# A new prologue for a two-layer attention and expert kernel: loads, splits, masks, sines and the first rotation in another order and place, and later x splits moved within their steps

## The chip, the cores and the metric

The kernel runs on one NeuronCore of a Trainium2 chip. Five engines run their own instruction streams and meet at semaphores: TensorE (PE), VectorE (DVE), ScalarE (ACT), GpSimd (POOL) and SyncE (SP), which here only issues DMAs. The metric is the device time of one execution in microseconds (us). Weights, activations and caches lie in HBM in float32.

## The reference, cut to what matters

For 8 batches of 128 tokens with 512 features, the first layer is attention over 512 cached and 128 new keys, with 32 query heads that share 8 key/value heads, and the second a linear layer with two gated low-rank experts per token.

```
q, k, v = x @ Wq.T, x @ Wk.T, x @ Wv.T            # 32 query heads, 8 key/value heads, D = 128
q, k = rmsnorm(q, q_norm_w), rmsnorm(k, k_norm_w)
pos = cache_seqlens[:, None] + arange(128)
q, k = rope(q, pos), rope(k, pos)                  # sines and cosines of pos * inv_freq
k_all = concat(k_cache[block_table], k); v_all = concat(v_cache[block_table], v)
scores = einsum(q, k_all) / sqrt(D); cached keys from cache_seqlens on are masked
x = x + softmax(scores) @ v_all @ Wo.T
x = x + x @ W.T + 2 * sum over the top 2 of 8 experts: gate * (x @ A_e.T) @ B_e.T
```

## The kernel before, in words

**Precision.** Every float32 matmul operand is split into a high part (a copy by ACT into the type float32r) and a low part (full minus high, by DVE, line 664). A product is three passes: high by high, low by high, high by low (lines 280 to 282). So all weights, x, queries, keys, probabilities and values go through ACT once and DVE once. The tiles have `_hi` and `_lo` in their names.

**Steps.** The work is numbered by g = 8 h + b, for key/value head h and batch b: 64 of them, one step each. It is software-pipelined by hand: step s computes the scores, softmax and transposed probabilities of g = s; the rotated queries and keys of g = s + 1; the projections Q and KV of g = s + 2; and the output of g = s - 1 (`O`, then `Y`, which DVE adds to the tile y, line 807). The loop runs from s = -2, so steps -2 and -1 are the prologue, and the text calls "step s" the stretch from the first scores matmul of step s (line 1011) to that of step s + 1. The order on every engine is the order of the code. Twelve outputs of PE a step (the list UNITS: `O`, `T0`, `Q` and so on) share the 4 PSUM banks of `ps_w` in turn.

**A step's loop over engines.** PE makes scores for 4 query heads; DVE takes each head's row maximum with the mask added (L727); ACT the exponential (L527); DVE the reciprocal of the sum (L734); ACT scales (L533); PE transposes (L1034); ACT and DVE split the transposed result (L538, L664). Beside it POOL takes the inverse norms for the next g (meansq L415, rstd L417, wr = norm weight times rstd L420), DVE scales by wr (u, L783), POOL multiplies by the cosine (L427), DVE by the sine (m2, L790), POOL adds the two halves (L434), and PE transposes the rotated queries (QT, L1102), the cached keys (KTC, L1019) and the new keys (KTN, L1113). Then the scores of the next step can start. POOL also issues four indirect DMAs per g that gather cached keys and values (L406).

**Weights of the next head.** W_AT and WO_AT say in which step a piece of the next head's weights is split: ACT at the end of step s (L478, L486), just ahead of the copy of KTN, DVE in step s + 1 after the second reciprocal; SP loads the piece a step before, as soon as DVE has freed the ring slot.

**x.** The transposed x of batch g is split once in head 0, kept in HBM (`keep_x`) and fetched again for later heads. The x of 4 batches is staged in half of y; when its splits are done, the natural x of those 4 batches is loaded over it (`natural_x`, L340), since Y is added to it.

**The prologue before.** Steps -2 and -1 hold all else that is done once: position angles and their reduction modulo 2 pi (L855 to L873), sines (L508, L509), masks of all 8 batches (L691), language biases (L697, 8 small ones), the splits of head 0's weights, which are loaded into tiles of later use, and the split of the first output weights wo (L493). ACT's order is: copy Q(0), two splits of wo, copy KV(0), squares. The gathers of g = 0 and 1 are issued by POOL ahead of all its arithmetic. ACT's copy of Q(1) (L589) waits for all 8 masks, because the key numbers from which they are made lie in the tile `raw`.

## Time and profile before

| | |
|---|---|
| median of 3 runs | 1195.59 us (1194.82 to 1195.92) |
| the profiled execution | 1195.48 us |
| its span (first to last instruction) | 1193.7 us |
| PE busy / DVE / ACT / POOL | 1155.7 / 928.4 / 938.9 / 768.2 us |
| first scores matmul | 34.66 us into the span |

The profile is of one execution. "Busy" for PE is modelled from pipelined matmuls. "Idle before, releaser" names the instruction whose semaphore ended a wait. A row of the timeline gives the start from the span's beginning, the duration, the engine, the line of the kernel and the operation. DVE and POOL instructions have their own records, so a duration that is much above that of its kind is read as a wait inside the instruction.

### The profile page before, as it was taken

How to read it: one execution, taken by the hardware profiler on the slowest of the kernel's cores; microseconds unless marked ns; L12 is line 12 of the kernel's file. 1: busy time of each engine (PE TensorE's matmuls, PEld its weight loads, DVE VectorE, ACT ScalarE, POOL GpSimd, SP SyncE). 2: the span in 40 equal slices, each digit the busy share in tenths (PEclk: the TensorE clock that was granted, in tenths of full speed). 3: DMA queues.
4: the chain of work that ended last, by engine and by line, in shares of the span. 5: the costliest groups of instructions: out<-in, count | busy, mean ns of one | idle time of the engine just before them, and what ended most of it. 6: DMA issues, size and time to landing. Idle time of an engine off the chain costs nothing.

```text
span 1193.7 us, 20774 instructions
## 1 busy us (share of the span) xinstructions
PE 1155.7 (97%) x6912; PEld 1025.5 (86%) x6912; DVE 928.4 (78%) x1880; ACT 938.9 (79%) x1830; POOL 768.2 (64%) x838
## 2 busy tenths in 40 slices
PE   3799999999999999999999999999999999999998
PEld 2688888888888888888888888888888888888787
DVE  6788887787878777887877787778878777877746
ACT  3787888888888888888888888888888888888741
POOL 5566666667677667676776766667667667666500
PEclk9899999999999999999999999999999999999999
DMA  6322412221222122122213222231222122121001
GB/s 237 119 85 96 146 61 80 94 93 48 93 94 76 64 93 94 53 88 93 90 51 94 93 67 74 93 94 49 92 93 81 58 92 91 55 69 54 18 1 71
DMA packets 53626, 98.11 MB, mean 82 GB/s; under 512 B 8592, under 2 KB 25872, under 8 KB 53264
## 3 DMA queue, kind: packets, MB, share of 16 engines
q1 hardware_dynamic: 41232, 63.21, 15.1%
q0 software_dynamic: 12288, 33.57, 9.5%
q8 instruction: 57, 0.93, 0.3%
q14 instruction: 49, 0.40, 0.1%
HBM read 90.45 MB, written 6.29 MB: 81 GB/s over the span
## 4 chain that ended last, share of the span: by engine, by line
PE 85%; DVE 5%; ACT 5%; issue 3%; DMA 1%; SPq 1%; POOL 0%; DVEq 0%; POOLq 0%; ACTq 0%
PE ps_s L1011 18%; PE ps_w L282 16%; PE ps_w L281 16%; PE ps_w L280 16%; PE ps_w L1034 8%; PE ps_w L1119 2%; PE ps_w L1102 2%; PE ps_s L993 2%; PE ps_w L1019 2%; ACT ps L527 2%; DVE pt_lo L664 2%; ACT ps L533 1%; DVE ps L727 1%; DMA y<-wo 1%; ACT pt_hi L538 1%
## 5 line engine op out<-in xcount | busy, mean ns | idle before, releaser
L406 POOL DMA_INDIRECT kv_raw<-kv,rows x256 | 254.0, 992 | 93.8 <-issue 62.7
L527 ACT ACTIVATE ps<-ps,negmax 128x640 f32<-128x640 f32 x256 | 211.9, 828 | 82.9 <-DVE negmax L727 49.4
L533 ACT ACTIVATE ps<-ps,recip 128x640 f32<-128x640 f32 x256 | 212.9, 832 | 71.0 <-DVE recip L734 52.9
L664 DVE TENSOR_TENSOR pt_lo<-ps_w,pt_hi 128x512 fp32r<-128x512 f32 x322 | 210.0, 684 | 58.5 <-ACT pt_hi L538 57.2
L727 DVE CUSTOM_DVE_ANT_0 ps<-ps_s,mask 128x640 f32<-128x640 f32 x256 | 206.6, 815 | 13.3 <-PE ps_s L1011 13.3
L280 PE MATMUL ps_w<-w_hi,xt_hi 128*128 128x512 f32 (+1 forms) x512 | 183.7, 359 | 11.5 <-DVE w_lo L664 8.2
L538 ACT ACTIVATE pt_hi<-ps_w 128x512 fp32r<-128x512 f32 x256 | 152.6, 596 | 27.8 <-PE ps_w L1034 21.5
L282 PE MATMUL ps_w<-w_hi,xt_lo 128*128 128x512 f32 (+1 forms) x512 | 173.2, 338 | 0.0
L281 PE MATMUL ps_w<-w_lo,xt_hi 128*128 128x512 f32 (+1 forms) x512 | 173.0, 338 | 0.0
L427 POOL TENSOR_TENSOR rot<-u,cos 128x640 f32<-128x640 f32 x64 | 101.8, 1591 | 110.0 <-DVE u L783 110.0
L1034 PE MATMUL ps_w<-cst,ps 128*128 128x128 f32 x1024 | 153.9, 273 | 7.1 <-DVE pt_lo L664 4.7
L434 POOL TENSOR_TENSOR rot<-rot,m 128x320 f32<-128x320 f32 x128 | 110.4, 884 | 51.3 <-DVE m L790 51.1
L1034 PEld LDWEIGHTS ps_w<-cst,ps 128*128 128x128 f32 x1024 | 124.5, 141 | 19.4 <-issue 10.4
L790 DVE TENSOR_TENSOR m<-u,sin 128x640 f32<-128x640 f32 x64 | 125.3, 1957 | 0.3 <-issue 0.3
L282 PE MATMUL ps_w<-pt_hi,v_lo 128*128 128x512 f32 x320 | 125.2, 391 | 0.0
L281 PE MATMUL ps_w<-pt_lo,v_hi 128*128 128x512 f32 x320 | 125.1, 391 | 0.0
L1011 PE MATMUL ps_s<-kt_hi,qt_hi 128*128 128x320 f32 x512 | 121.9, 319 | 3.2 <-DVE kt_lo L664 2.2
L280 PE MATMUL ps_w<-pt_hi,v_hi 128*128 128x512 f32 x320 | 124.9, 390 | 0.0
L1011 PE MATMUL ps_s<-kt_hi,qt_lo 128*128 128x320 f32 x512 | 117.5, 311 | 0.0
L1011 PE MATMUL ps_s<-kt_lo,qt_hi 128*128 128x320 f32 x512 | 117.4, 310 | 0.0
L280 PEld LDWEIGHTS ps_w<-w_hi,xt_hi 128*128 128x128 f32 x512 | 97.2, 190 | 20.8 <-DVE xt_lo L664 8.2
L1011 PEld LDWEIGHTS ps_s<-kt_hi,qt_hi 128*128 128x128 f32 x512 | 89.0, 189 | 25.3 <-issue 13.4
(155 smaller groups left out, 2583.1 us busy)
## 6 DMA issues: line engine op xcount, KB each, us to landing
xt_hi<-xsplit SPq DMA_DIRECT2D x56, 256.0 KB
xt_lo<-xsplit SPq DMA_DIRECT2D x56, 256.0 KB
w_raw<-wqkv SPq DMA_DIRECT2D x56, 192.0 KB
wo_raw<-wo SPq DMA_DIRECT2D x56, 128.0 KB
kv_raw<-kv,rows POOLq DMA_INDIRECT x256
xsplit<-xt_hi SPq DMA_DIRECT2D x8, 256.0 KB
xsplit<-xt_lo SPq DMA_DIRECT2D x8, 256.0 KB
y<-x SPq DMA_DIRECT2D x2, 1024.0 KB, 7.2
```

Source lines behind the costliest of these rows:

```text
L280: nc.tensor.matmul(out_ap, a_hi, b_hi, start=start and k == 0, stop=False)
L281: nc.tensor.matmul(out_ap, a_hi, b_lo, start=False, stop=False)
L282: last = nc.tensor.matmul(out_ap, a_lo, b_hi, start=False, stop=stop and k == n - 1)
L406: pool.indirect_dma_start(kv_raw[:, g % 2, t, :], None, kv[:, :], bass.IndirectOffsetOnAxis(rows[:, g % B, t:t + 1], 0)).then_inc(s_kv[g % ...
L527: nc.scalar.activation(ps[:, h, :], ps[:, h, :], ACT.Exp, bias=negmax[:, s % 2, h:h + 1], scale=-1.0, accum_out=rowsum[:, s % 2, h:h + 1]) ...
L533: nc.scalar.activation(ps[:, h, :], ps[:, h, :], ACT.Copy, scale=recip[:, s % 2, h:h + 1]).then_inc(a_norm, 1)
L538: nc.scalar.activation(pt_hi[:, 0:CT, h, :], bank(f"T{h}").rearrange("p (t q) -> p t q", t=CT), ACT.Copy).then_inc(a_pt, 1)
L664: return nc.vector.tensor_tensor(out_ap, full, hi.bitcast(F32), ALU.subtract)
L727: nc.vector.tensor_tensor_reduce(out=halves(ps[:, h, :]), in0=ps_s[:, h % 2, :, 0:KH], in1=halves(mask[:, b, :]), scale=-SCALE, scalar=3.0 ...
L790: nc.vector.tensor_tensor(m2[:], u[:], sin[:, g1 % B, :].unsqueeze(1).to_broadcast([P, NH, D]), ALU.mult).then_inc(d_m2, 1)
L1011: last = nc.tensor.matmul(ps_s[:, h % 2, half, 0:KH], a, c[:, half * KH:(half + 1) * KH], start=n == 0, stop=n == 2)
L1034: last = nc.tensor.transpose(bank(f"T{h}")[:, t * S:(t + 1) * S], ps[:, h, t * P:(t + 1) * P], ident)
```

## The change

The loop starts at s = 0, and each engine has a prologue written out by itself. In it:
- SP loads x in chunks, with the first 128-token chunk and the first weights ahead of the index and constant tables; the key numbers go to a part of `wo_raw` and not of `raw`, and come late; wo comes last, as before.
- POOL issues the gathers of g = 0 only when the key/value weights have landed, then takes rstd(0) and the cosine product, and then issues the gathers of g = 1.
- ACT goes through Q(0), KV(0) and the squares before any split of wo. The four splits of wo move into step 0 (two ahead of the first exponential, two after the second scaling).
- DVE interleaves the angles with the splits. For g = 0 it makes u with five instructions that multiply by rstd and the norm weight at once, so wr(0) isn't made, and it does the last additions of the rotation itself.
- DVE makes 2 of the 8 masks in the prologue, 2 in step 0, and 4 in step 1; the biases go to the end of step 8.
- The splits of x(2) and x(3) go into the still free part of `w_hi`/`w_lo` of head 1 and are done in the prologue and in step 0; in steps 2 to 5 DVE splits x(s+2) after the sums of squares and not at the end of the step before. ACT's part stays where it was.
- W_AT and WO_AT put the pieces of head 1's weights later: two w pieces in each of steps 1 to 4; wo pieces from step 2 on, two of them in steps 5 and 7.
- `natural_x(1)` is asked for in step 5 and not in step 4.

The number of matmuls and their order on PE stay.

```diff
-        W_AT.setdefault((0, 0, 1, 2, 2, 3, 4, 4)[j] if h == 1 else B * h - 11 + j, []).append((h - 1) * B + j)
-WO_AT = {s: [s] for s in range((HK - 1) * B + 2)}
+        W_AT.setdefault((1, 1, 2, 2, 3, 3, 4, 4)[j] if h == 1 else B * h - 11 + j, []).append((h - 1) * B + j)
+WO_AT = {2: [0], 3: [1], 4: [2], 5: [3, 4], 6: [5], 7: [6, 7]}
+for n in range(B, (HK - 1) * B + 2):
+    WO_AT[n] = [n]
...
+        def split_cols(g):
+            if 2 <= g < HB:
+                return w_hi[:, 1, (g + 2) * KC * S:(g + 3) * KC * S], w_lo[:, 1, (g + 2) * KC * S:(g + 3) * KC * S]
+            return xt_hi[:, g % 2, :], xt_lo[:, g % 2, :]
+
+        def xt_tile(part, g, k):
+            return split_cols(g)[part][:, k * S:(k + 1) * S]
...
+        kpos_stage = wo_raw[:].rearrange("p r n -> p (r n)")[:, 0:KEYS]
...
+                if n == 0:
+                    sp.wait_ge(d_mask, B)
...
+            w0 = wqkv[0].rearrange("p (k n) -> p k n", k=KC)
+            x_transposed(0, 0, 0, 1)
+            first_queries(0)
             sp.dma_start(cin[:], ints[:, :]).then_inc(s_ints, 16)
+            first_queries(1)
             sp.dma_start(cst[:], consts[:, :]).then_inc(s_cst, 16)
-            x_transposed(0, 0, 0, 2)
-            w0 = wqkv[0].rearrange("p (k n) -> p k n", k=KC)
-            for k in range(KC):
-                sp.dma_start(first_w(k), w0[:, k, 0:QW]).then_inc(s_w0[k], 16)
+            first_queries(2)
+            first_queries(3)
             sp.dma_start(first_kv, w0[:, :, QW:WW]).then_inc(s_w0kv, 16)
-            sp.dma_start(kpos_stage, kpos[:, :]).then_inc(s_tables, 16)
-            sp.dma_start(nw[:].rearrange("p h d -> p (h d)"), normw[:, :]).then_inc(s_tables, 16)
-            x_transposed(1, 0, 2, 4)
+            x_transposed(1, 0, 1, 2)
+            sp.dma_start(nw[:].rearrange("p h d -> p (h d)"), normw[:, :]).then_inc(s_nw, 16)
+            x_transposed(2, 0, 2, 4)
+            sp.dma_start(kpos_stage, kpos[:, :]).then_inc(s_kpos, 16)
             sp.dma_start(first_wo, wo[0]).then_inc(s_wo0, 16)
             keep_x(0)
             keep_x(1)
-            for s in range(-2, G):
+            for s in range(G):
                 for n in W_AT.get(s + 1, ()):
                     w_load(n)
                 for n in WO_AT.get(s + 1, ()):
                     wo_load(n)
                 if s == 0:
+                    keep_x(2)
+                    keep_x(3)
+                    natural_x(0)
                     sp.wait_ge(d_wolo, REP)
-                    x_transposed(2, 1, 0, 4)
-                if 2 <= s + 3 < B:
-                    keep_x(s + 3)
-                if s == 0 or s == HB:
-                    natural_x(s // HB)
+                    x_transposed(3, 1, 0, 4)
+                if HB <= s + 2 < B and s > 1:
+                    keep_x(s + 2)
+                if s == HB + 1:
+                    natural_x(1)
                 if B <= s + 4 < G:
                     fetch_x(s + 4)
...
+            pool.wait_ge(s_w0kv, 16)
+            gather_dma(0)
             pool.wait_ge(p_init, 2)
-            for s in range(-2, G + 1):
+            inverse_norms(0)
+            times_cosine(0)
+            gather_dma(1)
+            pool.wait_ge(s_nw, 16)
+            for s in range(G + 1):
                 step(s)
...
+                if c < 3 or c == HB:
+                    act.wait_ge(s_xt[min(c, 3)], 16)
+                if c >= HB:
                     wait(act, pe_kv, c - 2)
                     act.wait_ge(s_xkept[c % 2], 32 * (c // 2))
-                nc.scalar.activation(by_chunk(xt_hi[:, c % 2, :]), xt_stage(half, c % HB, c % HB + 1), ACT.Copy).then_inc(a_xhi, 1)
+                nc.scalar.activation(by_chunk(split_cols(c)[0]), xt_stage(half, c % HB, c % HB + 1), ACT.Copy).then_inc(a_xhi, 1)
...
+                elif n == B - 3:
+                    act.wait_ge(pe_kv, HB)
+                    act.wait_ge(s_xkept[0], 64)
+                    act.wait_ge(s_xkept[1], 64)
...
+                    if s > 0:
+                        keys_values(g1)
+                    squares(g1)
+                if s == 0:
+                    first_wo_split(0)
+                    first_wo_split(1)
...
+                if s == 0:
+                    first_wo_split(2)
+                    first_wo_split(3)
...
-                if s < 0:
-                    first_wo_split(2 * (s + 2))
-                    first_wo_split(2 * (s + 2) + 1)
-                if 2 <= s + 3 < B:
+                if HB <= s + 3 < B:
                     split_x(s + 3)
...
             split_x(0)
-            split_x(1)
...
-            for s in range(-2, G + 1):
+            split_x(1)
+            queries(0)
+            keys_values(0)
+            squares(0)
+            split_x(2)
+            split_x(3)
+            queries(1)
+            sines()
+            keys_values(1)
+            cached_keys(0)
+            turned_queries(0)
+            new_keys(0)
+            for s in range(G + 1):
                 step(s)
...
+                    if s < B and h == 0:
+                        dve.wait_ge(d_mask, s + 1)
...
+                if HB <= s + 2 < B and s > 1:
+                    split_x(s + 2)
...
+                if s < 2:
+                    masks(2 + 2 * s, HB + HB * s)
+                if s == 0:
+                    split_x(3)
+                    first_wo_split(0)
+                    first_wo_split(1)
                 for n in W_AT.get(s - 1, ()):
                     w_split(n)
...
+                if s == 0:
+                    first_wo_split(2)
+                    first_wo_split(3)
...
-                if s < 0:
-                    first_wo_split(2 * (s + 2))
-                    first_wo_split(2 * (s + 2) + 1)
-                if 2 <= s + 3 < B:
-                    split_x(s + 3)
+                if s == B:
+                    biases()
...
+            tab(nc.vector.memset(halfpi[:], float(np.pi / 2)))
+            split_x(0)
+            dve.wait_ge(s_ints, 16)
+            tab(nc.vector.tensor_copy(blkf[:].rearrange("p b t -> p (b t)"), cin[:, I_BLOCK:I_LEN]))
+            tab(nc.vector.tensor_copy(lenf[:], cin[:, I_LEN:I_LANG]))
+            tab(nc.vector.tensor_copy(langf[:], cin[:, I_LANG:I_END]))
+            first_w_low(0)
+            first_w_low(1)
+            dve.wait_ge(s_cst, 16)
+            tab(nc.vector.tensor_scalar(blkf[:], blkf[:], float(PSIZE), cst[:, C_SLOT:C_SLOT + 1], ALU.mult, ALU.add))
+            nc.vector.tensor_scalar(rows[:], blkf[:], -float(PAGES * PSIZE), None, ALU.add).then_inc(d_rows, 1)
+            tab(nc.vector.tensor_scalar(pos[:], lenf[:], cst[:, C_ROW:C_ROW + 1], None, ALU.add))
+            first_w_low(2)
             tab(nc.vector.tensor_tensor(ang, cst[:, C_INVF:C_INVF + HALF].unsqueeze(1).to_broadcast([P, B, HALF]),
                                         pos[:].unsqueeze(2).to_broadcast([P, B, HALF]), ALU.mult))
+            first_w_low(3)
             tab(nc.vector.tensor_scalar(whole, ang, float(1.0 / TWO_PI), None, ALU.mult))
             tab(nc.vector.tensor_copy(turns, whole))
-
-            split_x(0)
-            split_x(1)
-            wh, wl = head_weights(0)
-            for k in range(KC):
-                dve.wait_ge(a_whi, k + 1)
-                low(wl[:, k, 0:QW], first_w(k), wh[:, k, 0:QW]).then_inc(d_wlo, 1)
             for c in range(2):
                 dve.wait_ge(a_whi, KC + c + 1)
                 k = slice(c * KC // 2, (c + 1) * KC // 2)
                 low(wl[:, k, QW:WW], first_kv[:, k, :], wh[:, k, QW:WW]).then_inc(d_wlo, 1)
-            for part in (TWO_PI_A, TWO_PI_B, TWO_PI_C):
-                tab(nc.vector.scalar_tensor_tensor(out=ang, in0=turns, scalar=-part, in1=ang, op0=ALU.mult, op1=ALU.add))
+            split_x(1)
+            less_turns(TWO_PI_A)
+            less_turns(TWO_PI_B)
+            sums_of_squares(0)
+            less_turns(TWO_PI_C)
             tab(nc.vector.tensor_scalar(ang, ang, PI_BELOW, -PI_BELOW, ALU.min, ALU.max))
             nc.vector.scalar_tensor_tensor(out=absang, in0=ang, scalar=-1.0, in1=ang, op0=ALU.mult, op1=ALU.max).then_inc(d_ang, 1)
-            tab(nc.vector.tensor_copy(langf[:], cin[:, I_LANG:I_END]))
-            for s in range(-2, G + 1):
+
+            wait(dve, p_rstd, 0)
+            dve.wait_ge(s_nw, 16)
+            for h in range(NH):
+                ins = nc.vector.scalar_tensor_tensor(out=u[:, h, :], in0=raw[:, 0, h * D:(h + 1) * D], scalar=rstd[:, h:h + 1],
+                                                     in1=nw[:, h, :], op0=ALU.mult, op1=ALU.mult)
+            ins.then_inc(d_u, 1)
+            dve.wait_ge(a_sincos, 2)
+            nc.vector.tensor_scalar(sin[:, :, HALF:D], sin[:, :, 0:HALF], -1.0, None, ALU.mult).then_inc(d_tab, 1)
+            dve.wait_ge(d_tab, 1)
+            times_sine(0)
+            dve.wait_ge(d_m2, 1)
+            dve.wait_ge(p_m1, 1)
+            for a, c in ((0, HALF), (HALF, 0)):
+                nc.vector.tensor_tensor(rot[:, :, a:a + HALF], rot[:, :, a:a + HALF], m2[:, :, c:c + HALF],
+                                        ALU.add).then_inc(d_rot, 1)
+            cached_keys(0)
+            dve.wait_ge(s_kpos, 16)
+            masks(0, 1)
+            turned_queries(0)
+            new_keys(0)
+            masks(1, 2)
+            split_x(2)
+            for s in range(G + 1):
                 step(s)
...
-            for s in range(-2, G + 1):
-                if s == -1:
-                    pe.wait_ge(s_cst, 16)
+            project_queries(0)
+            project_keys_values(0)
+            project_queries(1)
+            project_keys_values(1)
+            pe.wait_ge(s_cst, 16)
+            turn_cached_keys(0)
+            turn_queries(0)
+            turn_new_keys(0)
+            for s in range(G + 1):
```

ACT, from its first splits to the first scores, before: Q(0) is copied, then wo is split, and KV(0) is copied.

```order
L634 ACTIVATE w_hi<-w_raw 128x2x256 x2
L589 ACTIVATE raw<-ps_w 128x512
L493 ACTIVATE wo_hi<-y 128x512 x2
L548 ACTIVATE raw<-ps_w 128x256
L555 ACTIVATE u<-raw 128x640
L508 ACTIVATE sin<-ps 128x8x64
L509 ACTIVATE cos<-ps,halfpi 128x512
```

And after, where L559 and L564 are the copies of Q and KV, L573 the squares, and L498 the split of x:

```order
L680 ACTIVATE w_hi<-w_raw 128x2x256 x2
L498 ACTIVATE xt_hi<-y 128x512
L559 ACTIVATE raw<-ps_w 128x512
L564 ACTIVATE raw<-ps_w 128x256
L573 ACTIVATE u<-raw 128x640
L498 ACTIVATE w_hi<-y 128x512 x2
L559 ACTIVATE raw<-ps_w 128x512
L543 ACTIVATE sin<-ps 128x8x64
```

The two splits of wo have gone from between the copies, and three splits of x stand in this stretch.

DVE in step 0 before, from the first sum's reciprocal to the last product of the rotation (L727 is the row maximum):

```order
L734 RECIPROCAL recip<-rowsum 128x1
L754 TENSOR_REDUCE sumsq<-u 128x5
L734 RECIPROCAL recip<-rowsum 128x1
L727 ISA ps,negmax<-ps_s,mask 128x640
L727 ISA negmax 128x1
L783 TENSOR_TENSOR u<-raw,wr 128x640
L734 RECIPROCAL recip<-rowsum 128x1
L790 TENSOR_TENSOR m<-u,sin 128x640
```

And after, where L819 is the reciprocal, L778 the sums of squares, L812 the row maximum:

```order
L819 RECIPROCAL recip<-rowsum 128x1
L778 TENSOR_REDUCE sumsq<-u 128x5
L819 RECIPROCAL recip<-rowsum 128x1
L749 TENSOR_SCALAR mask<-wo_raw,lenf 128x640 x2
L722 TENSOR_TENSOR w_lo<-y,w_hi 128x512
L722 TENSOR_TENSOR wo_lo<-y,wo_hi 128x512 x2
L812 ISA ps,negmax<-ps_s,mask 128x640
L812 ISA negmax 128x1
L862 TENSOR_TENSOR u<-raw,wr 128x640
```

Five instructions stand between the second reciprocal and the third row maximum.

SP around the load of the natural x of batches 4 to 7, before (the loop's pass s = 4: one w and one wo piece, the split x(7) kept, then y):

```order
L348 DMA w_raw<-wqkv 128x384
L355 DMA wo_raw<-wo 128x256
L326 DMA xsplit<-xt_hi 128x512
L327 DMA xsplit<-xt_lo 128x512
L340 DMA y<-x 128x4x512
L334 DMA xt_hi<-xsplit 128x512
L335 DMA xt_lo<-xsplit 128x512
```

And after, the end of pass 4 and the whole of pass 5 (L356 loads w, L365 wo, L335 keeps x, L342 and L343 fetch it):

```order
L342 DMA xt_hi<-xsplit 128x512
L343 DMA xt_lo<-xsplit 128x512
L356 DMA w_raw<-wqkv 128x384
L365 DMA wo_raw<-wo 128x256
L335 DMA xsplit<-xt_hi 128x512
L335 DMA xsplit<-xt_lo 128x512
L348 DMA y<-x 128x4x512
```

The load of y stands behind those of w piece 9 and wo piece 5, whose ring slots DVE frees in step 5.

## Rows read from the trace of the kernel before

**Rows 1.** The page: busy time by engine, and TensorE's granted clock in 40 slices.
```profile
PE 1155.7 (97%) x6912; PEld 1025.5 (86%) x6912; DVE 928.4 (78%) x1880; ACT 938.9 (79%) x1830; POOL 768.2 (64%) x838
PEclk9899999999999999999999999999999999999999
```

**Rows 2.** Stretches: length, busy PE, PEld, DVE, ACT, POOL, clock, DMA share, GB/s.
```profile
0.00:34.66 34.66, 12.63 (x57) 9.80 (x58) 23.93 (x49) 14.32 (x25) 17.61 (x22) 0.87 0.59 204
34.66:52.23 17.57, 13.96 (x77) 12.42 (x78) 12.18 (x25) 14.05 (x30) 9.47 (x11) 0.86 0.36 112
52.23:142.65 90.42, 87.94 (x520) 76.53 (x521) 75.35 (x143) 72.96 (x147) 59.50 (x66) 1.00 0.33 111
211.90:1077.48 865.58, 864.70 (x5200) 770.05 (x5201) 685.62 (x1349) 719.57 (x1399) 598.22 (x651) 1.00 0.25 80
```

**Rows 3.** The chain of waits, first 35 us: start, us, what.
```profile
7.25 11.92 DMA y<-wo
...
23.16 1.85 DVE mask L691 x4
...
27.45 2.18 POOL rot L427
...
29.70 2.06 POOL rot L434 x2
```

**Rows 4.** The timeline of the prologue: start, us, engine, line, operation, idle before.
```profile
8.24 0.77 PE L280 MATMUL ps_w<-w_hi,xt_hi 128*128 128x512 f32 x1 [8.24 <-DVE w_lo L664]
...
10.99 1.15 ACT L634 ACTIVATE w_hi<-w_raw 128x512 fp32r<-128x512 f32 x2 [0.86 <-DMA w_raw<-wqkv]
...
19.20 1.15 ACT L493 ACTIVATE wo_hi<-y 128x512 fp32r<-128x512 f32 x2 [5.48 <-DMA y<-wo]
...
20.67 0.39 PE L280 MATMUL ps_w<-w_hi,xt_hi 128*128 128x256 f32 x1 [3.24 <-ACT raw L548]
...
22.84 1.75 POOL L417 TENSOR_TENSOR rstd<-meansq,mhalf 128x5 f32<-128x5 f32 x1
```

**Rows 5.** Groups of the prologue: count, busy us, mean ns, idle before.
```profile
L406 POOL DMA_INDIRECT kv_raw<-kv,rows x8 | 8.6, 1080 | 2.5 <-issue 2.1 <-POOL rows L398 0.3
L871 DVE SCALAR_TENSOR_TENSOR ps<-ps 128x512 f32<-128x512 f32 x3 | 2.1, 689 | 0.1
L697 DVE TENSOR_SCALAR lang_bias<-cst,langf 128x8 f32<-128x8 f32 x8 | 1.8, 293 | 0.0
```

**Rows 6.** The timeline from 30 us on: copy of Q(1), first query transposes.
```profile
31.13 0.60 ACT L589 ACTIVATE raw<-ps_w 128x512 f32<-128x512 f32 x1 [7.10 <-DVE mask L691]
...
31.87 1.09 PE L1102 MATMUL ps_w<-cst,rot 128*128 128x128 f32 x4 [9.06 <-POOL rot L434]
```

**Rows 7.** The tile mask: its writer with shortest, median and longest ns.
```profile
L691 DVE TENSOR_SCALAR mask<-raw,lenf x8: 544/547/1820, 22.2 to 29.9; 128x640 bf16<-128x640 f32 x8
```

**Rows 8.** The timeline of step 2: second reciprocal, a wo split, POOL's wr.
```profile
76.09 0.17 DVE L734 RECIPROCAL recip<-rowsum 128x1 f32<-128x1 f32 x1 [0.97 <-ACT ps L527]
...
76.62 0.42 DVE L664 TENSOR_TENSOR wo_lo<-wo_raw,wo_hi 128x256 fp32r<-128x256 f32 x1
...
76.78 1.38 POOL L420 TENSOR_TENSOR wr<-nw,rstd 128x640 f32<-128x640 f32 x1
```

**Rows 9.** DVE's timeline around step 5 (124.53 to 142.65 us).
```profile
125.68 0.68 DVE L664 TENSOR_TENSOR xt_lo<-y,xt_hi 128x512 fp32r<-128x512 f32 x1
...
130.05 1.01 DVE L664 TENSOR_TENSOR w_lo<-w_raw,w_hi 128x384 fp32r<-128x384 f32 x2
130.97 1.48 DVE L664 TENSOR_TENSOR wo_lo<-wo_raw,wo_hi 128x256 fp32r<-128x256 f32 x1
...
138.79 0.67 DVE L807 TENSOR_TENSOR y<-ps_w,y 128x512 f32<-128x512 f32 x1
```

**Rows 10.** SP's timeline in step 5: the natural x of batches 4 to 7.
```profile
128.07 0.43 SPq L340 DMA_DIRECT2D y<-x  x1
```

**Rows 11.** DMA issues from 120 to 145 us: count, KB, us to landing.
```profile
y<-x SPq DMA_DIRECT2D x1, 1024.0 KB, 6.7
```

264 lines of the change are left out of this document (132 added, 132 removed).

## The prediction

> **What bounds the kernel now.** The page comes first: PE is busy 97% of the span and its clock is full but for the first slices [rows 1]. So the body of the program is read for what PE does, and the ends for who keeps PE waiting. The stretches say this step by step [rows 2]. Fifty later steps take 865.58 us, 17.31 each, with PE busy in all of them: there nothing but PE's work counts, and the change leaves that alone. Steps 1 to 5 take 90.42 us, 18.08 each, so 0.77 a step is lost to ACT and DVE, which carry head 1's splits there. Step 0 takes 17.57 although it has neither O nor Y, so it is a chain through DVE and ACT. The prologue takes 34.66 us, of which PE is busy 12.63. The chain in order of time names what it consists of: the load of wo (issued at 7.25, landed at 19.17), then masks and POOL's rotation [rows 3], and PE's transposes at 31.87. What can be won in whole microseconds is there; the rest of the change can only shift some tenths a step.
>
> **The prologue, part by part.** I build the new chain from the old durations.
>
> 1. *The wo wait.* Before, ACT's splits of wo stand between the copies of Q(0) and KV(0), and it waits 5.48 us for wo, until 19.20 [rows 4]. After, these copies don't stand behind it. What is late next is the key/value weights. They land at 10.98 before (end of a 0.86 us wait [rows 4]), when, by the shapes in the code, 2.2 MB had been asked for up to them, and gathers ran beside; after, it is 1.9 MB and no gathers: I take 9.8. ACT's two splits (1.15) end at 11.0, x(1) and Q(0) follow (1.2), KV(0) is copied at 13.0 to 13.4 once PE has it, squares end at 14.1, sums of squares at 15.0. Before, ACT began the squares only after wo's splits and KV(0)'s copy, about 1.5 after 19.20, so the sums ended at 22.2. This alone is 7.2 us.
> 2. *The first matmul.* It starts at 8.24, released by the low part of the first weights [rows 4], whose split stood behind two of x. With half as much x ahead, about 6.4. Worth little by itself, since the weights of keys and values decide.
> 3. *POOL.* Eight gathers took 8.6 + 2.5 us, 1.39 each [rows 5]. Four of them now start when the key/value weights land: 9.8 + 5.5 = 15.3, just past the sums of squares. rstd takes 0.4 + 1.75 [rows 4]: 17.4. If the weights landed 1 us later, all behind would too; this is the tightest point.
> 4. *The masks.* Six of 8 lie ahead of u on DVE in the chain (1.85 us of it [rows 3]), two more hold up the copy of Q(1) until 31.13 [rows 6] and with it the bank of the transposed queries. All that goes. wr (about 1.8 on POOL there) is replaced by five small DVE operations; the trace has none of that kind, the nearest is the same operation on 512 columns, 0.689 [rows 5]: at least 5 x 0.15, at most 5 x 0.69. I take 1.05, since the 128 columns are a quarter: u ends at 18.4.
> 5. *Rotation.* The sines are ready by 18.2 (angles at 16.8, then two activations of 512 columns, about 1.2 as in rows 4). The cosine product on POOL, with DVE's sine product falling into it, stood in the chain for 2.18, and the additions on POOL for 2.06 [rows 3]. After: a negation (0.4, under a mask's 0.547 [rows 7]), both products 2.3 together, so 21.1, and two additions on DVE of 0.45 each (320 columns, against 0.689 for 512 [rows 5]): 22.1.
> 6. *Transposes to scores.* From 31.87 to 34.66 are 2.79 [rows 6, 2] at half clock; 2.2 at full clock. DVE also has one mask in it (0.5), which fits into the wait for ACT. First scores at 24.3.
>
> Saved: 34.66 - 24.3 = **10.4 us**. Bounds: 12.5 if the weights land a microsecond earlier and the five operations are short, 8 if they land 1.5 later and the clock is half.
>
> **Steps 0 to 9, which pay for it.** An instruction that is put ahead of the third row maximum on DVE moves the whole rest of the step, unless a wait takes it.
>
> - *Step 0.* Ahead of the third maximum now stand two masks (0.5 each [rows 7]), the split of x(3) and two of wo (0.6 each): 2.8 us, and after the fourth maximum two more of wo (1.2, of which about 0.6 lies in a wait for ACT). They sit where POOL computes wr. The half clock of the first scores goes (0.9), DVE's next scores are not waited for, and DVE had about 1 us idle there. I take 18.4 for 17.57: **+0.8**; between -0.2 and +2.5.
> - *Step 1.* Four masks (1.9) between the second reciprocal and o_lo; before, two w and one wo split stood there (2.5, of them 1.48 for a wo split that elsewhere takes 0.42 [rows 8, 9]). The long one began while POOL's wr (1.38) ran, the short one before it [rows 8]. One mask took 1.82 against a median of 0.547, beside POOL's rotation [rows 7]. So I count one stall of 1.1 for the masks too. The split of x at the step's start goes (-0.6 on DVE). 18.5 for 18.04: **+0.5**; without the stall -0.6. The Trainium skill ("SBUF — State Buffer", section "SBUF: two separate sides") has this as a lock: a DVE operation in a 2-port mode, or with two SBUF inputs against a GpSimd operation that reads SBUF, and that GpSimd operation exclude each other for a whole instruction. By it the masks lose the 1.1; were it only shared bandwidth, step 1 would be 17.4 and the end 1186.8. The 1.82 and 1.48 speak for the lock.
> - *Steps 2 to 4.* DVE's split of x (0.68 in front of the first row maximum [rows 9]) goes behind the sums of squares, where DVE waits 0.97 us for the second exponential [rows 8]. It costs nothing there; ACT's second exponential hides it, and if that cover were gone it would cost its 0.6 again. ACT keeps two w splits a step. Step 2 has no wo on DVE: 17.45 for 18.07. Steps 3 and 4 have two w and one wo, with the stall: 17.95. Together **-0.9**.
> - *Step 5.* The natural x of batches 4 to 7 was issued at 128.07, 3.54 into step 5, and landed 6.7 later, at +10.2 [rows 10, 11]; DVE adds Y at +14.26 [rows 9]. After, the load stands behind wo piece 5, whose ring slot DVE frees with its third wo split, at about +7.2 in step 5 (before, the split ended at +7.9 [rows 9]); plus four issues (about 1.3) it goes out at +8.5 and lands at +15.2. The adder waits 1 to 1.5 us; behind it on DVE are the probabilities' low part, qt_lo and kt_lo, on which PE's next scores wait. DVE idles some 0.8 there, so 0.7 is left; with the moved x split saving 0.3, **+0.4**. At worst (7.7 and full queues) +2.
> - *Steps 6 to 8.* DVE splits two wo pieces where there was one in two of them, ACT likewise in steps 5 and 7: 0.42 each if nothing takes it [rows 8], 0.2 a step, **+0.6**; nothing to +1.5.
> - *Step 9.* Eight biases at the end of step 8: they took 1.8 us [rows 5], of which 0.6 was one stalled; 1.75 before the first row maximum. These steps have some 0.4 of slack over PE's 17.31: **+1.3**; 0 to +1.8.
>
> Sum of the steps: +0.8 + 0.5 - 0.9 + 0.4 + 0.6 + 1.3 = +2.7. The tail is the same. The profiled execution took 1195.48, 1.8 around its span of 1193.7; 1195.48 - 10.4 + 2.7 = 1187.8. That execution is 0.11 under the median of 1195.59, so 1187.9, or **1188**.
>
> **Rivals.**
>
> *The clock falls in the new gap.* In the trace PE is idle 3.24 us before 20.67 and its 256-column matmul still takes 0.39 [rows 4], at the full 2.4 GHz; it is idle 9.06 before 31.87 [rows 6], and step 0, with 0.86 granted [rows 2], begins at 1.2 GHz. The new gap, from the transposes of the cached keys to 22.1, is about 4.5 us, between the two. If it falls, transposes cost 0.6 more, scores 0.7, as before the change: 1189.3. For it: the gap is longer than that which was survived. Against: it is half the other. It lies in my range.
>
> *Later steps don't pay.* The moved masks, splits and biases lie in ACT's and DVE's gaps, since both are busy under 85% of steps 1 to 5 [rows 2]. Then the +2.7 is about -0.5 and the time 1184.6. For it: some 3 us idle a step on each. Against: steps 1 to 5 were already late with the same share idle, so the gaps don't lie where they would help.
>
> *The prologue gains half.* POOL's gathers now wait for the weights; if these land at 12.5 and POOL ends at 18, rstd is at 20, scores at 27: 1190.6. With it a late y: 1192.
>
> *Slower.* The scores of step 0 need head 0's data alone, but one mechanism reaches further: ring slots. SP's queue is in order, and now w and wo pieces wait on DVE steps behind which keep_x, the natural x and the fetch of x(8) stand. If that fetch came late, Q(8) in step 6 would stop PE. It needs x at +6.5 of step 6; it is issued when KV(6) is done, at +16 of step 4, in both kernels, so there are 8 us for 512 KB. To lose more than the 7.7 of the sum, each of steps 3 to 8 would have to wait 1.3 us for SP; it decides from transfers of over 8 us on, against 6.7 for a whole megabyte [rows 11]. Time then about 1197.
>
> **Chances.** Forecast (1186 to 1189.5, with or without the fall of the clock, which I give 1 in 2) 0.58; later steps free 0.17; half the prologue 0.20; slower 0.03; other 0.02. What a measurement can tell from no change is 0.2%, 2.4 us, so faster is under 1193.2: 0.95; same 0.03; slower 0.02. The range takes the forecast and most of both neighbours: 1183.5 to 1191.5.
>
> **What would show it.** In the new profile: first scores matmul at 24.3 (22.5 to 26.5); squares begun at 13.4; POOL's first gather right after the weights, rstd ending near 17.4; a granted clock under 1 between 22 and 38 us or not; steps 0 and 1 at 18.4 and 18.5, 2 at 17.45, 3 and 4 at 17.95, 5 at 18.5 with a DVE wait for `y<-x`, 9 at 18.6, and 17.31 from 10 on. I am wrong if the first scores come after 27 us, or if the steps up to 9 sum to under 177.2 (their old sum, 17.57 + 90.42 + four at 17.31).

## The result, and the profile after

The changed kernel takes 1191.57 us (median of 7 runs, 1191.05 to 1192.51) beside 1195.7 for the kernel before on the same chip: the ratio is 0.9966, with a 95% interval of 0.9955 to 0.9977. It is faster, by 4.1 us and not by the 7.7 of the forecast, and lies just above the forecast's range of 1183.5 to 1191.5. Run again beside three experiments it took 1192.50 against 1196.00, ratio 0.9970 (0.9958 to 0.9982).

The page of the changed kernel has the same picture as before [rows 1]: PE at 97%, and the clock short of full at the start alone.

```profile
PE 1157.0 (97%) x6912; PEld 1027.2 (86%) x6912; DVE 932.6 (78%) x1886; ACT 942.1 (79%) x1830; POOL 764.8 (64%) x835
...
PEclk8999999999999999999999999999999999999999
```

The stretches, cut at the first scores matmul, at the end of step 0, at the end of step 5 and at the start of step 10 (columns as in [rows 2]; the last one holds 50 steps again):

```profile
0.00:26.42 26.42, 13.40 (x57) 9.88 (x58) 18.42 (x38) 14.82 (x26) 11.96 (x19) 0.89 0.73 253
26.42:47.24 20.82, 15.11 (x77) 13.79 (x78) 17.40 (x30) 13.26 (x26) 11.62 (x12) 0.81 0.41 129
47.24:137.07 89.83, 87.10 (x521) 76.93 (x521) 74.62 (x144) 75.00 (x149) 62.70 (x67) 1.00 0.34 108
207.83:1073.40 865.57, 864.47 (x5202) 770.17 (x5201) 687.49 (x1349) 721.73 (x1399) 597.27 (x651) 1.00 0.25 80
```

The prologue is 8.24 us shorter (26.42 for 34.66), step 0 is 3.25 longer (20.82 for 17.57) and at a lower clock than before, 0.81 for 0.86. Fifty later steps take 865.57, as before. From the first scores matmul of one step to that of the next, read from PE's timeline:

| step | 0 | 1 | 2 | 3 | 4 | 5 | 6 | 7 | 8 | 9 | 10 |
|---|---|---|---|---|---|---|---|---|---|---|---|
| before | 17.57 | 18.04 | 18.07 | 18.11 | 18.08 | 18.12 | 17.32 | 17.31 | 17.31 | 17.31 | 17.31 |
| forecast | 18.4 | 18.5 | 17.45 | 17.95 | 17.95 | 18.5 | 17.5 | 17.5 | 17.5 | 18.6 | 17.31 |
| after | 20.82 | 18.41 | 17.49 | 17.50 | 17.49 | 18.94 | 17.66 | 17.38 | 17.60 | 18.12 | 17.31 |

Steps 0 to 9 sum to 181.41 against 177.24, so they give back 4.17 of the 8.24. The difference, 4.07, is the whole of the measured gain.

**The prologue.** The timeline of all engines (start, us, engine, line, operation, output and inputs, count, idle time before and its releaser):

```profile
10.83 1.15 ACT L680 ACTIVATE w_hi<-w_raw 128x512 fp32r<-128x512 f32 x2 [1.05 <-DMA w_raw<-wqkv]
...
15.82 0.82 DVE L778 TENSOR_REDUCE sumsq<-u 128x5 f32<-128x640 f32 x1 [0.48 <-ACT u L573]
...
17.39 1.38 POOL L436 TENSOR_TENSOR rstd<-meansq,mhalf 128x5 f32<-128x5 f32 x1
...
18.81 1.40 DVE L954 SCALAR_TENSOR_TENSOR u<-raw,rstd,nw 128x128 f32<-128x128 f32 x5 [0.38 <-POOL rstd L436]
...
20.58 2.04 DVE L785 TENSOR_TENSOR m<-u,sin 128x640 f32<-128x640 f32 x1
...
22.66 0.89 DVE L964 TENSOR_TENSOR rot<-rot,m 128x320 f32<-128x320 f32 x2
...
23.60 1.12 PE L1129 MATMUL ps_w<-cst,rot 128*128 128x128 f32 x4 [1.12 <-DVE rot L964]
...
26.42 0.87 PE L1157 MATMUL ps_s<-kt_hi,qt_hi 128*128 128x320 f32 x2 [1.49 <-DVE kt_lo L722]
```

The wait for wo [rows 4] and the nine microseconds of PE's wait for POOL [rows 6] are gone, and the chain is the one forecast: weights of keys and values (10.83), sums of squares (15.82), rstd (17.39), u, the products, the additions. It runs a little late at each link, and PE is at half clock (1.2 GHz): four transposes take 1.12, where at full clock they take 0.60. The clock had fallen before them: PE was idle for 2.69 us ahead of the transposes of the cached keys at 21.39, which waited for the gathered keys and took 1.09.

**Step 0.** Here is the loss. The kernel before had, on DVE, ACT and PE:

```profile
40.93 0.81 DVE L727 CUSTOM_DVE_ANT_0 ps<-ps_s,mask 128x640 f32<-128x640 f32 x1
...
42.99 0.82 ACT L527 ACTIVATE ps<-ps,negmax 128x640 f32<-128x640 f32 x1
...
47.42 0.63 PE L1034 MATMUL ps_w<-cst,ps 128*128 128x128 f32 x4 [2.63 <-DVE pt_lo L664]
```

that is the third row maximum 6.27 us into the step and the third exponential 8.33 into it. After:

```profile
32.62 0.16 DVE L819 RECIPROCAL recip<-rowsum 128x1 f32<-128x1 f32 x1 [0.99 <-ACT ps L593]
...
32.70 1.00 DVE L749 TENSOR_SCALAR mask<-wo_raw,lenf 128x640 bf16<-128x640 f32 x2
...
33.35 1.46 POOL L456 TENSOR_TENSOR wr<-nw,rstd 128x640 f32<-128x640 f32 x1
...
33.61 1.75 DVE L722 TENSOR_TENSOR w_lo<-y,w_hi 128x512 fp32r<-128x512 f32 x1
...
35.28 1.28 DVE L722 TENSOR_TENSOR wo_lo<-y,wo_hi 128x512 fp32r<-128x512 f32 x2
...
36.49 0.81 DVE L812 CUSTOM_DVE_ANT_0 ps<-ps_s,mask 128x640 f32<-128x640 f32 x1
...
37.34 0.83 ACT L593 ACTIVATE ps<-ps,negmax 128x640 f32<-128x640 f32 x1 [1.45 <-DVE negmax L812]
...
41.83 1.09 PE L1166 MATMUL ps_w<-cst,ps 128*128 128x128 f32 x4 [5.28 <-DVE pt_lo L722]
```

The second reciprocal (32.62, +6.20) is where it was. Behind it two masks, the low split of x(3) (its names are `w_lo<-y,w_hi`, since x(3) lies in the second weight buffer) and two of wo take 3.8 us, and the row maximum begins at +10.07. The x split takes 1.75 where the others take 0.68: it was begun at 33.61, while POOL's wr ran from 33.35 to 34.81. PE waits 5.28 us for what follows (2.63 before), and after that its four transposes take 1.09, at half clock. The step is best read in two parts, cut where this wait ends, 12.76 us into the step before and 15.41 after. So 2.65 of the loss of 3.25 are there by then. The other 0.60 come behind it, where 4.81 us at a clock of 1.00 have become 5.41 at 0.73 (mean granted clock of these stretches).

**Steps 3 and 5.** Rows of DVE and POOL of step 3, then SP's load and DVE's addition of Y in step 5:

```profile
87.03 0.68 DVE L722 TENSOR_TENSOR xt_lo<-y,xt_hi 128x512 fp32r<-128x512 f32 x1
87.20 0.57 POOL L434 TENSOR_SCALAR meansq<-sumsq 128x5 f32<-128x5 f32 x1 [1.19 <-DVE sumsq L778]
...
89.10 0.42 DVE L722 TENSOR_TENSOR wo_lo<-wo_raw,wo_hi 128x256 fp32r<-128x256 f32 x1
89.14 1.49 POOL L456 TENSOR_TENSOR wr<-nw,rstd 128x640 f32<-128x640 f32 x1
...
125.85 0.48 SPq L348 DMA_DIRECT2D y<-x  x1
...
133.63 0.69 DVE L883 TENSOR_TENSOR y<-ps_w,y 128x512 f32<-128x512 f32 x1 [2.50 <-DMA y<-x]
```

The wo split of step 3 begins 0.04 us ahead of POOL's wr and takes 0.42; in the kernel before it began within it and took 1.48 (in step 3 as in step 5 [rows 9]). The rows above say how it got there. The x split in its new place runs from 87.03, POOL's mean squares begin inside it and take 0.57, where they take 0.20 otherwise, and so wr begins later: 1.05 behind DVE's second reciprocal (88.09). In the kernel before it was 0.69 behind it. In step 5 the natural x is issued at +7.72, lands at +15.5, and the addition waits 2.50 us for it.

### The profile page after: what moved, and what is told of

The parts are those of the page before. It is cut to its first block, busy times and chain, and to the rows that moved or that the text cites. A ratio compares the mean times of both kernels' runs of the same rounds, so it can differ in the third digit from the quotient of the medians.

```text
span 1189.5 us, 20784 instructions
## 1 busy us (share of the span) xinstructions
PE 1157.0 (97%) x6912; PEld 1027.2 (86%) x6912; DVE 932.6 (78%) x1886; ACT 942.1 (79%) x1830; POOL 764.8 (64%) x835
## 4 chain that ended last, share of the span: by engine, by line
PE 87%; DVE 6%; ACT 3%; issue 2%; DMA 1%; SPq 0%; POOL 0%; DVEq 0%; ACTq 0%; POOLq 0%
PE ps_s L1157 18%; PE ps_w L290 17%; PE ps_w L288 17%; PE ps_w L289 17%; PE ps_w L1166 9%; PE ps_w L1227 2%; PE ps_w L1129 2%; PE ps_w L1136 2%; PE ps_s L1091 2%; ACT ps L593 2%; DVE pt_lo L722 1%; DVE ps L812 1%; ACT ps L599 1%; DMA y<-x 1%; DVE w_lo L722 1%
## 5 line engine op out<-in xcount | busy, mean ns | idle before, releaser
L812 DVE CUSTOM_DVE_ANT_0 ps<-ps_s,mask 128x640 f32<-128x640 f32 x256 | 204.0, 815 | 1.8 <-PE ps_s L1157 1.8
L288 PE MATMUL ps_w<-w_hi,xt_hi 128*128 128x512 f32 x496 | 178.0, 359 | 9.1 <-DVE w_lo L722 7.6
L290 PE MATMUL ps_w<-w_hi,xt_lo 128*128 128x512 f32 x496 | 167.7, 338 | 0.0
L289 PE MATMUL ps_w<-w_lo,xt_hi 128*128 128x512 f32 x496 | 167.4, 337 | 0.0
L785 DVE TENSOR_TENSOR m<-u,sin 128x640 f32<-128x640 f32 x64 | 128.1, 2001 | 0.0
L819 DVE RECIPROCAL recip<-rowsum 128x1 f32<-128x1 f32 x256 | 40.9, 160 | 92.7 <-ACT ps L593 92.5
```

Of the source, the lines that this page charges most:

```text
L288: nc.tensor.matmul(out_ap, a_hi, b_hi, start=start and k == 0, stop=False)
L289: nc.tensor.matmul(out_ap, a_hi, b_lo, start=False, stop=False)
L290: last = nc.tensor.matmul(out_ap, a_lo, b_hi, start=False, stop=stop and k == n - 1)
L785: nc.vector.tensor_tensor(m2[:], u[:], sin[:, g % B, :].unsqueeze(1).to_broadcast([P, NH, D]), ALU.mult).then_inc(d_m2, 1)
L812: nc.vector.tensor_tensor_reduce(out=halves(ps[:, h, :]), in0=ps_s[:, h % 2, :, 0:KH], in1=halves(mask[:, b, :]), scale=-SCALE, scalar=3.0 ...
```

## The experiments

Each edit below is against the changed kernel, and each was timed beside the kernel before. "Scores" is the first scores matmul, "step 10" the start of step 10 (211.90 in the kernel before), both from the profiled execution; the ratio is to the kernel before.

| kernel | scores | step 0 | 1 | 2 | 3 | 4 | 5 | 9 | step 10 | time | ratio (95%) |
|---|---|---|---|---|---|---|---|---|---|---|---|
| changed | 26.42 | 20.82 | 18.41 | 17.49 | 17.50 | 17.49 | 18.94 | 18.12 | 207.83 | 1191.57 | 0.9966 (.9955-.9977) |
| e8_again | 26.09 | 21.11 | 18.31 | 17.49 | 17.48 | 17.48 | 19.16 | 18.12 | 208.45 | 1192.50 | 0.9970 (.9958-.9982) |
| e1_step0 | 25.96 | 19.10 | 18.50 | 17.50 | 17.49 | 17.50 | 18.88 | 18.13 | 205.68 | 1189.86 | 0.9948 (.9935-.9962) |
| e2_fill | 26.09 | 19.47 | 18.54 | 17.48 | 17.48 | 17.48 | 18.89 | 18.12 | 206.17 | 1189.91 | 0.9945 (.9932-.9959) |
| e3_natx | 27.00 | 21.27 | 18.41 | 17.49 | 17.50 | 17.48 | 17.38 | 18.13 | 207.24 | 1190.03 | 0.9948 (.9935-.9962) |
| e4_bias | 26.21 | 21.96 | 18.61 | 17.48 | 17.48 | 17.48 | 18.49 | 17.31 | 207.64 | 1191.28 | 0.9956 (.9943-.9970) |
| e5_gath | 25.82 | 21.70 | 18.50 | 17.48 | 17.48 | 17.48 | 18.60 | 18.12 | 207.88 | 1191.64 | 0.9962 (.9949-.9976) |
| e6_rotd | 26.14 | 20.87 | 18.50 | 17.49 | 17.48 | 17.49 | 18.65 | 18.12 | 207.47 | 1191.34 | 0.9961 (.9947-.9974) |
| e7_hold | 25.89 | 20.75 | 18.49 | 17.50 | 17.49 | 17.71 | 19.07 | 18.12 | 207.71 | 1192.61 | 0.9970 (.9957-.9982) |
| e9_room | 26.00 | 19.83 | 18.42 | 17.49 | 17.48 | 17.48 | 18.72 | 18.13 | 206.17 | 1190.16 | 0.9953 (.9940-.9967) |
| e10_roomfill | 26.58 | 18.68 | 18.40 | 17.49 | 17.48 | 17.49 | 18.81 | 18.11 | 205.66 | 1188.13 | 0.9935 (.9922-.9949) |
| e11_all | 25.72 | 17.49 | 18.59 | 17.48 | 17.50 | 17.49 | 17.39 | 17.31 | 201.55 | 1185.21 | 0.9913 (.9899-.9926) |
| e12_xback | 25.75 | 21.85 | 18.31 | 17.97 | 18.54 | 18.54 | 21.63 | 18.12 | 213.52 | 1196.38 | 1.0003 (.9994-1.0012) |

Where step 0 is left as it is (the changed kernel, its repetition, e3 to e7, e12) it takes between 20.75 and 21.96, and the first scores come between 25.75 and 27.00. So a single trace tells the start of the scores to about 0.6 us either way, while steps 2 to 4 repeat to 0.02 in all but e7 and e12. Step 0 is steadier than it looks. In all eight of these traces TensorE's long wait ends 15.40 or 15.41 us into it; what varies is the part behind, 5.34 to 6.55 us, with the granted clock (0.73 and 0.54 at the two ends). Cut there, the kernels are:

| step 0 | before | changed | e2_fill | e1_step0 | e9_room | e10_roomfill | e11_all |
|---|---|---|---|---|---|---|---|
| until the wait ends | 12.76 | 15.41 | 14.17 | 13.15 | 14.27 | 13.17 | 13.10 |
| from there to the next scores | 4.81 | 5.41 | 5.30 | 5.95 | 5.56 | 5.51 | 4.39 |

The changed kernel was not run beside e1 to e4 or e9 to e12, and the intervals of e1 to e4 and e9 overlap with its own. There the sizes below are those of single traces. e10, e11 and e12 lie clear of it.

**e8_again.** The changed kernel itself.

> The changed kernel itself, on the chip of the three others, to have its time and a second trace beside theirs. Theory A (the long step 0 is made by the order of VectorE's instructions and repeats): first scores at 26.2 to 26.6, step 0 at 20.8 to 21.9 (the profiles of two kernels that leave it as it is have 21.27 and 21.96), the third row maximum at 10.07 into the step, and steps 1 to 9 within 0.1 of the first trace but for step 5. Theory B (what differs between executions is as large as what is to be explained): step 0 at 18 to 19.5 in this execution.

Theory A holds: step 0 took 21.11. Its third row maximum begins at 36.15, +10.06, behind the same 1.00, 1.75 and 1.28, to 0.01 us. Step 5 was longer (19.16), and so was step 6, which the theory had not allowed: 18.15 for 17.66, and no cause of it was found.

**e1_step0.** VectorE's order in step 0.

```diff
-            masks(1, 2)
+            masks(1, 4)
 # step(0): first_wo_split(0) between rowmax(0) and rowmax(1), split_x(3) behind sums_of_squares
-                if s < 2:
-                    masks(2 + 2 * s, HB + HB * s)
-                if s == 0:
-                    split_x(3)
-                    first_wo_split(0)
-                    first_wo_split(1)
+                if s == 1:
+                    masks(4, B)
 # at the end of step 0: first_wo_split(1), (2) and (3)
```

> Against the changed kernel: of what VectorE has ahead of the third row maximum of step 0, two masks go ahead of the step, the split of x(3) behind the sums of squares, the first split of wo between the first two row maxima, the second to the end of the step. Nothing is left out. Theory A (the order on VectorE): the third row maximum, which begins 10.07 us into the step in the changed kernel and 6.27 in the kernel before, comes back to 6.3 to 6.9; TensorE then waits about 2.6 us in the step instead of 5.28, so its clock may hold at the end of the step as well; step 0 takes 17.5 to 18.0 instead of 20.82 and the time falls by 3.0, to 1188.5. Theory B (the clock): the step is long because TensorE runs at half clock at both of its ends; then step 0 stays above 20 and the time above 1190.8. Theory C (the moved work is only shifted): the instructions at the end of the step hold up the transposed keys and queries instead, step 0 about 19.5 and 1190.2.

The third row maximum came back to +6.28, as theory A said, and the x split takes 0.68 in its new place. But the step took 19.10, nearest to the 19.5 of theory C. Rows of DVE, ACT and PE:

```profile
32.24 0.81 DVE L812 CUSTOM_DVE_ANT_0 ps<-ps_s,mask 128x640 f32<-128x640 f32 x1
...
35.34 0.82 ACT L593 ACTIVATE ps<-ps,negmax 128x640 f32<-128x640 f32 x1
...
39.11 0.63 PE L1167 MATMUL ps_w<-cst,ps 128*128 128x128 f32 x4 [3.02 <-DVE pt_lo L722]
```

The exponential stands at +9.38, 2.4 us after its maximum: ACT has two wo splits (1.14), the probabilities and the value split ahead of it, without a pause. Before the change that exponential was at +8.33, with no wo in that place. So ACT is a second, parallel price that DVE's had hidden, but a small one: of its 1.05, 0.67 come back, because the sine product now begins later beside POOL's cosine product and takes 1.26 for 1.93, and the wait ends 0.39 later than before the change. The other 1.14 stand behind the wait (5.95 for 4.81), at a granted clock of 0.71. Theory C's hold-up is not what made them, since TensorE is idle there for 0.35 us, less than the 0.61 before the change. The DVE order was worth 1.7 of the 3.25; theory B (all of it the clock) is out; most of what is left is the clock.

**e2_fill.** TensorE kept busy in the prologue.

```diff
+            def fill(n):
+                for _ in range(n):
+                    nc.tensor.matmul(ps_s[:, 1, 1, :], w_hi[:, 0, 0:P], xt_hi[:, 1, 0:512], start=True, stop=True)
+            fill(11)
             turn_cached_keys(0)
+            fill(6)
             turn_queries(0)
             turn_new_keys(0)
+            fill(5)
```

> Against the changed kernel: TensorE gets 22 more matmuls of 512 columns in the prologue (11 ahead of the transposes of the cached keys, 6 ahead of those of the queries, 5 behind those of the new keys), into a bank that the scores overwrite. Theory A (the clock falls in the idle gap): the granted clock stays full from 13 us to the first scores; transposes of the queries take 0.60 instead of 1.12, scores begin 0.5 to 0.7 us sooner than 26.42, the first two heads' scores take 0.29 instead of 0.535 a pair, so the second row maximum of step 0 comes 1.4 us sooner in the step, and step 0, in which nothing else of it changes, takes 19.6 instead of 20.82: in all 1.8 us, to 1189.8. Theory B (the clock doesn't matter, the chain is VectorE's): first scores 0.5 sooner, step 0 unchanged within 0.3: 1191.0. Theory C (the added matmuls themselves hold up the transposes): first scores at 26.4 or later, 1191.5 or more.

The stretches of this kernel (20 us to the scores, the scores to 34 us, 34 us to the end of step 0) and of the changed one:

```profile
20.00:26.09 6.09, 5.27 (x26) 3.58 (x25) 5.70 (x11) 3.85 (x8) 4.92 (x4) 1.00 0.32 104
26.09:34.00 7.91, 6.87 (x38) 5.84 (x39) 6.45 (x13) 6.08 (x12) 4.37 (x5) 1.00 0.32 102
34.00:45.56 11.56, 6.29 (x41) 5.83 (x41) 11.06 (x18) 7.05 (x15) 7.50 (x8) 0.85 0.54 161
```

```profile
20.00:26.42 6.42, 2.42 (x9) 1.67 (x10) 5.58 (x10) 3.74 (x8) 5.05 (x5) 0.56 0.27 96
26.42:34.00 7.58, 7.15 (x30) 6.60 (x31) 4.75 (x12) 4.51 (x9) 3.19 (x4) 0.69 0.32 107
34.00:47.24 13.24, 7.96 (x49) 7.20 (x48) 12.64 (x19) 8.76 (x18) 8.44 (x9) 0.87 0.45 142
```

The granted clock is the column behind POOL: 1.00 and 1.00 with the fill where it was 0.56 and 0.69. The first scores came 0.33 sooner (0.45, counted from the additions of the rotation), step 0 was 1.35 shorter: 1.7 together, as theory A had it. So the half clock up to there costs 1.7 us even though the chain is not PE's, mostly through the second row maximum, which waits for 12 score matmuls at 0.27 each instead of 0.15.

**e3_natx.** The natural x ahead of the weights' loads.

```diff
             for s in range(G):
+                if s == HB + 1:
+                    keep_x(s + 2)
+                    natural_x(1)
                 for n in W_AT.get(s + 1, ()):
```

> Against the changed kernel: the sixth pass of the DMA queue's program issues the keeping of x(7) and the load of the natural x of batches 4 to 7 ahead of the loads of weights, where it issued them behind. Nothing is left out. Theory A (the addition of Y waits for that load): it lands 1.5 to 3 us sooner, VectorE's addition of Y in step 5 falls from 15.50 into the step to 13.6, as in step 4, and step 5 takes 17.5 instead of 18.94; the time falls by 1.4, to 1190.2. Theory B (step 5 is long for another reason, such as the two wo splits of ACT): step 5 stays at 18.5 or more and the time within 0.4 of 1191.6. Theory C (the loads of weights come late instead): step 5 falls to 17.5, steps 6 and 7 lose as much.

```profile
124.64 1.10 SPq L348 DMA_DIRECT2D y<-x  x1
...
132.82 0.69 DVE L884 TENSOR_TENSOR y<-ps_w,y 128x512 f32<-128x512 f32 x1 [0.67 <-PE ps_w L290]
```

Issued at +5.49, it is there in time: the addition is at +13.67 and its 0.67 of idle time is PE's. Step 5 takes 17.38 for 18.94, and steps 6 to 8 don't change. Theory A, to 0.1.

**e4_bias.** One bias a step.

```diff
-                if s == B:
-                    biases()
 # behind sums_of_squares(g1):
+                if B < s <= 2 * B:
+                    biases(s - B - 1, s - B)
```

> Against the changed kernel: the eight biases stand one a step in steps 9 to 16, behind the sums of squares, where VectorE waits 0.97 us for an exponential, and no longer all at the end of step 8. Nothing is left out. Theory A: step 9 takes 17.3 instead of 18.12 and steps 10 to 16 stay at 17.31: the time falls by 0.8, to 1190.8. Theory B (each bias costs its 0.15 to 0.22 us in its step, or stalls beside GpSimd): steps 9 to 16 take 17.4 to 17.5 each and nothing is won.

Step 9 takes 17.31, and so do steps 10 to 15, each to 0.01: theory A. The time (1191.28, where 1190.8 was forecast) doesn't tell 0.8 us, and this trace can't be summed up either: its step 0 was the longest seen (21.96).

**e5_gath and e7_hold.** What sets the arrival of the key and value weights. In the one GpSimd's gathers don't wait for them, in the other nothing more is loaded until they are there.

```diff
-            pool.wait_ge(s_w0kv, 16)      # e5_gath
             gather_dma(0)
+            sp.wait_ge(s_w0kv, 16)        # e7_hold
             x_transposed(2, 0, 2, 4)
```

> Against the changed kernel: GpSimd's first four gathers don't wait for the weights of keys and values. Nothing is left out. In the changed kernel these weights are there at 10.83 us and the gathers run from 11.10 to 16.2, 0.65 us before GpSimd is released by the sums of squares. Theory A (the gathers are off the chain, and cost the weights nothing): the gathers run from 8.5 to 13.5, the weights are there at 10.8 to 11.0, first scores at 26.2 to 26.5 and the time within 0.3 of the changed kernel's. Theory B (the gathers take the weights' bandwidth): the weights come 1 us later and the first scores at 27.4 or later, the time 1 us above. Theory C (the gathers did hold back the inverse norms): first scores sooner by 0.5.

> Against the changed kernel: the DMA queue's program waits until the weights of keys and values have landed before it issues the load of x(2) and x(3), of the key numbers and of wo, and the keeping of x(0). Nothing is left out. Theory A (transfers issued later share the bandwidth with the earlier ones): the weights are there at 9.5 to 10 us instead of 10.83 and the first scores come at 25.5; wo lands at about 21, which nothing waits for, and the time falls by 0.9. Theory B (the transfers end in the order of their issue, the rate is what it is): the weights come at 10.8, the first scores at 26.4 or, should x(2) or the key numbers be late, after 27.

ACT's split of these weights, in the two kernels:

```profile
10.76 1.15 ACT L679 ACTIVATE w_hi<-w_raw 128x512 fp32r<-128x512 f32 x2 [1.60 <-DMA w_raw<-wqkv]
```

```profile
10.78 1.15 ACT L681 ACTIVATE w_hi<-w_raw 128x512 fp32r<-128x512 f32 x2 [1.18 <-DMA w_raw<-wqkv]
```

10.76 and 10.78 for 10.83, where the kernels that leave these loads alone have 10.36 to 11.21. So the microsecond that the forecast counted on comes neither from taking the gathers away nor from holding back the loads behind; less than about 0.4 us these traces can't tell. For e5 theory A holds on the weights, and for e7 theory B. The first scores came sooner than either had it (25.82 and 25.89), within the spread named above. Theory C of e5 (the gathers held back the inverse norms) had such a time, but u begins 2.98 us behind the start of the sums of squares in e5 and 2.99 in the changed kernel, so it is out. The forecast's "1.9 MB and no gathers: I take 9.8" is not borne out: the weights were there 0.16 sooner than before.

**e6_rotd.** Both products of the first rotation on VectorE.

```diff
             inverse_norms(0)
-            times_cosine(0)
             gather_dma(1)
+            nc.vector.tensor_tensor(rot[:]..., u[:]..., cos[:, 0, :]..., ALU.mult).then_inc(p_m1, 1)
             times_sine(0)
```

> Against the changed kernel: the cosine product of the first rotation stands on VectorE, ahead of its sine product, and no longer on GpSimd beside it. Nothing is left out. In the changed kernel the sine product takes 2.04 us beside GpSimd's cosine product of 1.65, from 20.29 to 22.62. Theory A (a VectorE instruction and a GpSimd instruction shut each other out of memory, so the two ran one after the other): both products take 0.8 each on VectorE, the additions begin at 22.1 instead of 22.66, and the time falls by 0.5. Theory B (the sine product takes 2.0 by itself): the additions begin at 23.3 and the time rises by 0.6. Theory C: GpSimd's gathers of batch 1, which now run there, stretch both products: nothing is won.

```profile
21.21 0.83 DVE L959 TENSOR_TENSOR rot<-u,cos 128x640 f32<-128x640 f32 x1
...
21.96 0.82 DVE L784 TENSOR_TENSOR m<-u,sin 128x640 f32<-128x640 f32 x1
...
22.81 0.89 DVE L967 TENSOR_TENSOR rot<-rot,m 128x320 f32<-128x320 f32 x2
```

0.83 and 0.82, where the sine product alone took 2.04 beside POOL's 1.65. From the negation (20.13 in the changed kernel, 20.76 here) to the additions it is 2.05 instead of 2.53. Theory A, 0.5 us. The time (1191.34, beside 1192.50 for the changed kernel) has the right sign, but the intervals overlap. The trace's first scores don't show it, since its sums of squares began 0.64 later (16.46 for 15.82).

**e9_room and e10_roomfill.** Room in step 0 on two engines, and the clock on top.

```diff
 # ACT, prologue: first_wo_split(0), (1) ahead of cached_keys(0); step(0): (2), (3) ahead of exps(0)
 # DVE, prologue: masks(0, 2) ahead of turned_queries(0), masks(2, 4) behind new_keys(0)
 # DVE, step(0): split_x(3) behind sums_of_squares
                 if has(s):
                     rowmax(2)
+                if s == 0:
+                    first_wo_split(0)
+                    first_wo_split(1)
 # first_wo_split(2) ahead of over_sum(2), (3) behind over_sum(3)
 # PE, e10_roomfill: the fill of e2_fill, and behind turn_probs(1) of step 0
+                    pe.wait_ge(d_max, 3)
+                    for _ in range(9):
+                        nc.tensor.matmul(ps_s[:, 0, 0, :], w_hi[:, 0, 0:P], xt_hi[:, 1, 0:512], start=True, stop=True)
```

> Against the changed kernel, step 0 once more, now on two engines. ScalarE splits the first half of wo in the prologue, ahead of the copy of the cached keys, the second half ahead of step 0's first exponential, so that nothing of wo stands ahead of the third one. VectorE has masks 2 and 3 ahead of the step, the split of x(3) behind the sums of squares, two low splits of wo in its wait for GpSimd's wr, one ahead of the third reciprocal, one at the end. Nothing is left out. Where only VectorE's order was changed the third row maximum came back to +6.28, but the third exponential stood at +9.38 behind 1.14 us of wo and the step took 19.10. Theory A (each engine's queue ahead of the third exponential is the price): the exponential at +8.2 to 8.4, as before the change (8.33), the fourth row maximum at 11.2, and step 0 at 17.8 to 18.3; the time at 1188.9 to 1189.4 where the changed kernel has 1192. Theory B (GpSimd's wr and the rotation behind it set the end of the step): 18.9 or more.

> The kernel with room in step 0, and with the 22 added matmuls in the prologue and nine more behind the transposes of the second head of step 0, where TensorE waits. Nothing is left out. Theory A (the clock's price adds to that of the order): the granted clock is full from 13 us to the end of step 0; first scores 0.3 sooner, step 0 at 16.3 to 17.0: with the prologue 1.5 under the kernel with room alone, 1187.6. Theory B (with its order mended the step is VectorE's and ScalarE's chain, and the clock is worth only what the first two heads' scores save, 0.7 or less).

The third exponential is at +8.33, as in the kernel before, and still step 0 of e9 took 19.83, more than e1. The forecast for it failed, and the rows say why:

```profile
33.01 2.35 DVE L721 TENSOR_TENSOR wo_lo<-y,wo_hi 128x512 fp32r<-128x512 f32 x2
...
33.23 1.58 POOL L456 TENSOR_TENSOR wr<-nw,rstd 128x640 f32<-128x640 f32 x1
...
36.62 0.15 DVE L818 RECIPROCAL recip<-rowsum 128x1 f32<-128x1 f32 x1
```

I had put two wo splits into DVE's wait for wr. That wait exists because POOL computes wr just then, so the second split stood still until wr was done: 2.35 instead of 1.28, and u began at +9.28 instead of +8.13. With one more split (0.68) ahead of it the third reciprocal came at +10.62 instead of +9.26. A wait for POOL's arithmetic is no free place for DVE operations that read two tiles of SBUF. The number lies in the range of theory B (18.9 or more), but TensorE's long wait ends with DVE's low part of the probabilities and not with POOL's rotation. In e10 step 0 took 18.68, which is theory A's sign and only part of its size (16.3 to 17.0 expected): the clock was full until +13.6 only and 0.66 from there on, and the stall was the same. Its first scores came at 26.58 and not 0.3 sooner than in e9 (26.00); its weights came 0.10 later, and the rest stays open.

**e11_all.** e10_roomfill with e3, e4 and e6.

> All edits that gained, together: room in step 0, the added matmuls, the natural x of batches 4 to 7 ahead of the weights' loads, one bias a step, the cosine product of the first rotation on VectorE. Nothing is left out. If the gains add: first scores at 25.2 to 25.6, step 0 at 16.3 to 17.0, step 5 at 17.4, step 9 at 17.3: 1.5 + 0.8 + 0.4 under the kernel with room and added matmuls, about 1185. If the edits take each other's slack: within 1 us of that kernel.

1185.21 us (1185.04 to 1186.13), ratio 0.9913 (0.9899 to 0.9926): 10.9 us under the kernel before where the change had 4.1, with intervals well apart. First scores 25.72, step 5 17.39, step 9 17.31; the gains add. The sum came out as forecast (about 1185), its first two terms did not: the scores were expected at 25.2 to 25.6 and step 0 at 16.3 to 17.0. Step 0 took 17.49, 1.2 less than in e10 with the same instructions in it, which no theory had. PE's transposes behind its wait, of e10 and of e11:

```profile
40.22 0.79 PE L1130 MATMUL ps_w<-cst,rot 128*128 128x128 f32 x4
...
40.79 1.06 PE L1137 MATMUL ps_w<-cst,kv_raw 128*128 128x128 f32 x4
```

```profile
38.82 0.63 PE L1171 MATMUL ps_w<-cst,ps 128*128 128x128 f32 x4 [2.11 <-DVE pt_lo L721]
...
39.28 0.60 PE L1134 MATMUL ps_w<-cst,rot 128*128 128x128 f32 x4
...
39.72 0.60 PE L1141 MATMUL ps_w<-cst,kv_raw 128*128 128x128 f32 x4
```

Both kernels idle 2.11 us there. In one the clock fell (0.79, 1.06), in the other it held (0.60, 0.60).

**e12_xback.** The x splits at their old place in steps 2 to 5.

```diff
+                if HB <= s + 2 < B and s > 1:
+                    split_x(s + 2)
                 if has(s):
                     rowmax(0)
                     rowmax(1)
                     over_sum(0)
                 if has(g1):
                     sums_of_squares(g1)
-                if HB <= s + 2 < B and s > 1:
-                    split_x(s + 2)
```

> Against the changed kernel: VectorE's low splits of x(4) to x(7) stand ahead of the first row maximum of steps 2 to 5 again, as in the kernel before, and not behind the sums of squares. Nothing is left out. Theory A (this move is what made steps 2 to 4 shorter): they take 18.1 each again instead of 17.49, step 5 about 0.3 more: 2.1 us in all. Theory B (the new order of the weights' loads and splits did it): they stay at 17.5 to 17.6. Theory C (half each): 17.8.

Theory A, and twice its size: the whole gain of the change is gone (1196.38, ratio 1.0003; its eleven times spread from 1195.21 to 1198.07, and the trace is of 1197.46). Step 2, where DVE splits no wo, takes 17.97, steps 3 and 4 take 18.54. Rows of step 3, then the addition of Y in step 5:

```profile
85.03 0.68 DVE L722 TENSOR_TENSOR xt_lo<-y,xt_hi 128x512 fp32r<-128x512 f32 x1
...
88.44 0.20 POOL L434 TENSOR_SCALAR meansq<-sumsq 128x5 f32<-128x5 f32 x1 [1.56 <-DVE sumsq L778]
...
90.00 1.51 POOL L456 TENSOR_TENSOR wr<-nw,rstd 128x640 f32<-128x640 f32 x1
...
90.32 1.48 DVE L722 TENSOR_TENSOR wo_lo<-wo_raw,wo_hi 128x256 fp32r<-128x256 f32 x1
...
137.81 0.69 DVE L883 TENSOR_TENSOR y<-ps_w,y 128x512 f32<-128x512 f32 x1 [2.52 <-DMA y<-x]
```

The wo split stands 1.0 us behind the second reciprocal in both kernels (89.32 here, 88.09 in the changed one). It is POOL's wr that has moved: with no x split beside them the mean squares take 0.20 for 0.57, wr begins 0.68 behind that reciprocal for 1.05, and the wo split falls inside it and takes 1.48 for 0.42. So the split's own place costs 0.48 (step 2), and with the stall it is 1.05 (steps 3 and 4). At 18.54 they are longer than the 18.1 of the kernel before, so the rest of the change costs 0.4 in each of them; that it is the new order of the weights is likely and not shown. Step 5's load stands behind that step's wo split, so it is issued at 130.22, +9.26. DVE waits 2.52 us for it, as long as in the changed kernel, but later in the step; TensorE waits 2.28 for 1.37 and falls to a clock of 0.58 behind it, and step 5 takes 21.63.

## Why the prediction was wrong, point by point

The start of step 10 was forecast at 24.3 + 179.9 = 204.2 and came at 207.83. The 3.6 us between are:

- **Step 0 is the step that failed: +3.25, forecast +0.8, and beyond its own bounds (-0.2 to +2.5).** "Ahead of the third maximum now stand ... 2.8 us" was the right mechanism. It was 3.8: the sum left out the stall of the x split beside wr (1.07), though it placed the group "where POOL computes wr". The idle time that it took off was there: DVE's old wait of 1.04 for wr was absorbed, and 3.8 late at the third maximum was 2.65 at the fourth and at the end of TensorE's wait. The figures of the sum don't make +0.8 either: 2.8 and 0.6, less 0.9 and about 1, are +1.5, and what took off the rest stands on no row. The 0.9 that it took off for a full clock was not: the clock fell, at the start of the step as before the change, and once more in the longer wait, which added 0.60 at its end. e1 gave back 1.7 of it by DVE's order, e2 1.35 by the clock. ACT's wo splits ahead of the third exponential I hadn't priced at all; they only show once DVE's price is gone, and then as 0.39 of their 1.05. No run takes them away alone. The two wo splits behind the fourth maximum, forecast at 1.2, took 2.53 beside POOL, and cost nothing, since TensorE had work by then.
- **The prologue: 8.24 saved, forecast 10.4 (8 to 12.5).** Weights at 10.83 and not 9.8 (1.0); e5 and e7 leave no ground for 9.8. Five small operations took 1.40 for 1.05. Half clock from the transposes on: 2.87 from the additions to the scores for 2.2. The gathers were not "the tightest point": POOL was idle 0.65 before the sums.
- **Steps 2 to 4: -1.78, forecast -0.9.** Better than forecast. I had kept the 1.1 stall in steps 3 and 4. It went, by a path that the forecast didn't have: the moved x split holds POOL's mean squares for 0.37, wr begins that much later, and the wo split is ahead of it by 0.04 us. That is luck and not foresight. e12 shows both parts: 0.48 from the split's old place, and 1.05 where the stall comes with it.
- **Step 5: +0.82, forecast +0.4.** The wait for the natural x, as forecast. It was issued at +7.72 (I had 8.5), took 7.8 us and not 6.7, and cost 2.50 of wait. e3 takes it away.
- **Steps 1 and 6 to 8: +0.37 and +0.70, forecast +0.5 and +0.6.** Right. The masks of step 1 took 2.92 for four: the one stall.
- **Step 9: +0.81, forecast +1.3.** Right in kind. The eight biases took 1.16 and not 1.75; the forecast had kept the 0.6 of one stalled bias. What the slack took is 0.35, as forecast (0.4).
- **The lock.** What I gave in the sum a stall of 1.1, on the rows of one mask and one split, is shown by e6 (0.83 and 0.82 against 2.04 beside 1.65), e9 and e12: a DVE operation with two inputs in SBUF that begins within one of POOL's operations waits for its end, and one that begins 0.04 us before it does not. The masks, with one such input, were held too (one of step 1 took 1.55), and POOL is held in its turn (0.57 for 0.20). The low part of the probabilities, one of whose inputs lies in PSUM, is not held: two took 1.27 at 41.01, while POOL's additions ran from 40.48 to 42.16. The Trainium skill ("SBUF — State Buffer", section "SBUF: two separate sides") has this rule: whichever of the two starts first keeps the other out for the whole instruction, if the DVE operation has two SBUF inputs and POOL's reads SBUF. The trace agrees.

Of the rivals the fall of the clock came true and costs 1.7, not 1.3. It fell in a gap of 2.69 us, shorter than the 3.24 that it had survived before the change, and in e9 it was still full behind one of 3.70 (four transposes in 0.63), so the rival's comparison of gaps by their length alone doesn't hold. "Later steps don't pay" and the slots of SP's ring did not. The step sum came above 177.2, the first scores before 27: by its own marks the forecast was right in structure, and wrong in the size of step 0.

## What to carry over

When instructions are moved ahead of a point in an in-order queue, price them at that point, and take off idle time only if it lies between their new place and that point. Ask for each what the other engine that shares the memory runs at that moment: a shift of 0.37 us in POOL's queue gave or took a microsecond here. And ask whether a second engine has the same wait behind the first, since undoing one price shows the next.

## What was not expected of the hardware

- How sharp the edge of the stall is: 0.42 us for a split begun at 89.10 with POOL's operation at 89.14, 1.48 for one begun at 90.32 with POOL's at 90.00.
- A DVE split moved behind the sums of squares made a later split shorter, by 1.06 us, since it delayed POOL's arithmetic between the two.
- 512 KB of weights were there at 10.76 with gathers beside them, at 10.78 with the 1.9 MB of loads behind them held back, and at 10.83 in the changed kernel, which does neither; by the spread of the traces that is the same.
- The clock fell in one and held in the other of two kernels with the same instructions in step 0 and the same 2.11 us of idle time on TensorE (e10, e11). What tells them apart stays open.
- The addition of matmuls whose results nobody uses made a kernel faster, though PE is busy 97% of the span: 22 of them by 1.7 us (e2), 31 by 2.0 (1190.16 to 1188.13, e9 to e10).
